# Silu by tanh in late shared experts, and final tiles moved among shared tiles, in a one-core mixture-of-experts kernel

## What is computed

```python
# cond: two shared experts, and eight routed ones of which two count for a token
for e in range(2):
    h = silu(x @ s_w1[e].T) * (x @ s_w3[e].T)
    shared = shared + h @ s_w2[e].T
for e in range(8):
    h = gelu(x @ r_w1[e].T, approximate=False)
    routed = routed + h @ r_w2[e].T * gates[:, e:e + 1]
c = (shared / 2 + routed) / 4
# ffn, of low rank
P = c @ U1
H = gelu_tanh(P @ V1 + b1)
out = (H @ U2) @ V2 + b2
```

## Time and profile before

| | |
|---|---|
| median of three runs | 882.41 us |
| the profiled execution | 882.33 us |
| its span, first to last instruction | 880.1 us |
| PE busy, 3838 matmuls | 868.8 us, 99% |
| DVE, ACT, POOL busy | 675.8, 573.0, 404.3 us |
| granted PE clock, mean | 0.999 |

### The profile page before, as it was taken

One profiled execution on the slowest core, in us unless ns is written; L12 is line 12 of the kernel. 1 busy time (PEld: TensorE's weight loads), 2 busy tenths in 40 slices (PEclk: granted clock), 3 DMA queues, 4 the chain that ended last, 5 costly groups with the idle time before them and its releaser, 6 DMA issues.

```text
span 880.1 us, 12608 instructions
## 1 busy us (share of the span) xinstructions
PE 868.8 (99%) x3838; PEld 691.6 (79%) x3838; DVE 675.8 (77%) x1091; ACT 573.0 (65%) x1029; POOL 404.3 (46%) x377
## 2 busy tenths in 40 slices
PE   8999999999999999999999999999999999999997
PEld 5787888778888888888888888888888887777874
DVE  7877777878689687686687686686665788998887
ACT  7888888755555455555555555555555678989796
POOL 7457783134356453252252252352324427754462
PEclk9999999999999999999999999999999999999999
DMA  9689981023113112012012012011010038462700
GB/s 322 216 270 308 298 288 46 1 86 136 49 48 124 43 42 84 1 48 84 1 49 83 1 49 84 0 48 49 1 48 1 1 122 211 91 182 58 158 13 36
DMA packets 36547, 83.21 MB, mean 95 GB/s; under 512 B 4480, under 2 KB 14592, under 8 KB 34688
## 3 DMA queue, kind: packets, MB, share of 16 engines
q1 hardware_dynamic: 36192, 82.15, 29.3%
q10 hardware_dynamic: 288, 0.26, 0.1%
HBM read 71.39 MB, written 6.83 MB: 89 GB/s over the span
## 4 chain that ended last, share of the span: by engine, by line
PE 70%; DVE 2%; issue 2%; ACT 2%; POOL 0%; POOLq 0%; DVEq 0%; ACTq 0%
PE ps L933 15%; PE ps L952 15%; PE ps L938 15%; PE ps L993 6%; PE ps L995 6%; PE ps L988 6%; PE ps L975 2%; PE ps L973 2%; DVE Hf L1575 1%; ACT HH L1093 1%; PE ps L968 1%; DVE HL L1588 1%; DVE HH L1585 0%; ACT Hf L1080 0%; POOL HL L1683 0%
## 5 line engine op out<-in xcount | busy, mean ns | idle before, releaser
L1087 ACT ACTIVATE Sg<-ps 128x512 f32<-128x512 f32 x288 | 171.8, 597 | 245.9 <-PE ps L952 245.3
L1568 DVE TENSOR_TENSOR Hf<-ps,Sg 128x512 f32<-128x512 f32 x288 | 198.0, 688 | 148.9 <-ACT Sg L1087 92.4
L1683 POOL TENSOR_TENSOR HL<-Hf,HH 128x512 fp32r<-128x512 f32 x133 | 177.7, 1344 | 174.5 <-ACT HH L1093 158.4
L1093 ACT ACTIVATE HH<-Hf 128x512 fp32r<-128x512 f32 x344 | 215.0, 625 | 14.2 <-DVE Hf L1568 9.8
L1588 DVE TENSOR_TENSOR HL<-Hf,HH 128x512 fp32r<-128x512 f32 x243 | 214.1, 881 | 4.3 <-ACT HH L1093 3.2
L933 PE MATMUL ps<-XHL,WBH 128*128 128x512 f32 x512 | 203.5, 397 | 0.5 <-DVE Hf L1568 0.5
L952 PE MATMUL ps<-XHL,WBH 128*128 128x512 f32 x512 | 202.1, 395 | 0.0
L938 PE MATMUL ps<-XHL,WBL 128*128 128x512 f32 x512 | 202.0, 395 | 0.0
L1698 POOL TENSOR_TENSOR XT<-XT,TMP 128x512 f32<-128x512 f32 x64 | 83.8, 1310 | 223.3 <-DVE TMP L1435 223.1
L933 PEld LDWEIGHTS ps<-XHL,WBH 128*128 128x128 f32 x512 | 96.0, 188 | 24.6 <-DVE Hf L1568 1.6
L952 PEld LDWEIGHTS ps<-XHL,WBH 128*128 128x128 f32 x512 | 96.0, 188 | 23.0
(11 more groups left out here) (261 smaller groups left out, 1325.3 us busy)
## 6 DMA issues: line engine op xcount, KB each, us to landing
CWB<-scratch SPq DMA_DIRECT2D x14, 1024.0 KB, 4.6
GWD<-expert_down SPq DMA_DIRECT2D x21, 576.5 KB, 4.6
GWU<-expert_up SPq DMA_DIRECT2D x21, 514.0 KB, 5.2
CWB<-scratch SPq DMA_DIRECT2D x40, 256.0 KB, 5.9
ST<-in_wb_dram SPq DMA_DIRECT2D x8, 768.0 KB, 6.3
ST<-scratch SPq DMA_DIRECT2D x24, 256.0 KB, 8.8
GX<-XT SPq DMA_DIRECT2D x68, 64.0 KB, 2.9
XT<-in_x_dram SPq DMA_DIRECT2D x8, 256.0 KB, 5.7
```

Of the source, the lines that this page charges most:

```text
L1087: e.activation(Sg[:, it.n % NG, :], zb[z % NZ][:, :], ACT.Silu).then_inc(s_act, 1)
L1093: e.activation(HH[:, it.n % NH, 0:it.cols], hidden_place(it), ACT.Copy).then_inc(s_hi_act, 1)
L1568: e.tensor_tensor(Hf[:, it.n % NS, :], zb[z % NZ][:, :], Sg[:, it.n % NG, :], ALU.mult).then_inc(s_prod, 1)
L1683: e.tensor_tensor(HL[:, it.n % NH, :], Hf[:, it.n % NS, :], HH[:, it.n % NH, :].bitcast(F32), ALU.subtract).then_inc(s_lo_pool, 1)
```

## The change

- `LATE` is 6 and `MIXED` is 4. At the end stand only (5, 2), (5, 3) and blocks 6 and 7: ten final tiles. (5, 0) and (5, 1) come before the routed tiles of pair 6.
- In pairs 4 and 6 the four final tiles of block b - 2 stand among the shared tiles, as S S F S S F S S F S S F. The final tiles of block b - 1 follow (four in pair 4, two in pair 6), then the routed ones. Pair 2 keeps its order.
- Whole are only (5, 3), (6, 1), (6, 3), (7, 1), (7, 3). Before, they were these and (2, 3), (3, 3), (5, 1).
- Final tiles of blocks 2 and 4 are `among`: their gelu stays in the PSUM bank, ACT makes the high part, DVE the low part, and the bank is free when that low part is made. They use no `Hf` buffer, so `hf_free` passes over them.
- Shared tiles of blocks 4 to 7 are `tanh`: ACT writes tanh(z / 2), DVE makes (tanh + 1) times z in place, which frees the gate's bank, waits for that, and multiplies by the up half. This is twice the silu, so `FOLD` scales the shared part by 0.0625. The shared tiles of blocks 0 to 3 keep the silu, and their product gets a factor of 2 by another kind of instruction.
- The low parts of all shared tiles from block 2 on are POOL's; before, blocks 2 and 3 alone. Low parts of final tiles 1 and 3 of blocks 2 to 4, as far as they had one, go from POOL to DVE. Of the final tiles at the end, the one low part that is POOL's is that of (7, 0) and no longer of (6, 0).

```diff
@@ -15,7 +15,8 @@
 BLK = 512
 NBLK = NT // BLK
 SEG = (0, 42, 86, 128)
-LATE = NBLK - 3
+LATE = NBLK - 2
+MIXED = 4
 LAG = 5
 NH = LAG + 1
 NS = 6
@@ -72,8 +73,11 @@
         self.kind, self.blk, self.ex, self.f, self.last = kind, blk, ex, f, last
         self.cols = GROUPS[blk][1] * P if kind == "G" else BLK
 
-        self.whole = kind == "F" and (f % 2 == 1 if blk >= LATE else blk in (2, 3) and f == 3)
-        self.inplace = kind in "AG"
+        self.late = kind == "F" and (blk, f) >= (LATE - 1, 2)
+        self.whole = self.late and f % 2 == 1
+        self.among = kind == "F" and blk in range(MIXED - 2, LATE, 2)
+        self.inplace = kind in "AG" or self.among
+        self.tanh = kind == "S" and blk >= MIXED
 
 
 class Order:
@@ -111,13 +115,12 @@
         return [Item("F", blk, 0, f, f == 3) for f in range(4)]
 
     for b in range(0, NBLK, 2):
-        items += shared(b) + shared(b + 1)
-        for f in (b - 2, b - 1):
-            if 0 <= f < LATE:
-                items += final(f)
-        items += routed(b) + routed(b + 1)
-    for b in range(LATE, NBLK):
-        items += final(b)
+        mixed = {"S": shared(b) + shared(b + 1), "F": final(b - 2) if b else []}
+        for kind in "SSFSSFSSFSSF" if b >= MIXED else "SSSSSSSS" + "FFFF" * (b > 0):
+            items.append(mixed[kind].pop(0))
+        items += ([it for it in final(b - 1) if not it.late] if b else []) + routed(b) + routed(b + 1)
+    for b in range(LATE - 1, NBLK):
+        items += [it for it in final(b) if it.late]
     return items
 
 
@@ -223,6 +226,7 @@
         s_small = sem("s_small")
         s_act = sem("s_act")
         s_prod = sem("s_prod")
+        s_half = sem("s_half")
         s_gated = sem("s_gated")
         s_hi_act, s_hi_dve = sem("s_hi_act"), sem("s_hi_dve")
         s_lo_dve, s_lo_pool = sem("s_lo_dve"), sem("s_lo_pool")
@@ -345,12 +349,14 @@
                 for j in range(2 if it.kind in "BS" else 1):
                     it.z.append(len(z_users))
                     z_users.append((it, j))
-        n_prod, n_gated = {}, {}
+        n_prod, n_gated, n_half = {}, {}, {}
         hi, lo = {}, {}
         n_hi_act = n_hi_dve = n_lo_dve = n_lo_pool = 0
         for it in real:
             if it.kind in "BS":
                 n_prod[it.n] = len(n_prod) + 1
+            if it.tanh:
+                n_half[it.n] = len(n_half) + 1
             if it.kind == "R":
                 n_gated[it.n] = len(n_gated) + 1
             if it.whole:
@@ -358,10 +364,10 @@
                 lo[it.n] = s_down, it.n + 1
                 continue
             it.hi_act = it.kind in "BS" or (it.kind in "AG" and it.k % (8 if it.k < 16 else 4) != 0) or (
-                it.kind == "F" and it.blk < LATE and it.k % 2 == 1) or (it.kind == "R" and it.ex % 4 != 3)
+                it.among or (it.kind == "F" and not it.late and it.f % 2 == 1)) or (it.kind == "R" and it.ex % 4 != 3)
             it.lo_pool = (it.kind == "B" and it.k % 4 in ((1, 3) if it.ex == 7 and it.blk > 2 else (1,))) or (
-                it.kind == "F" and ((it.blk, it.f) == (LATE + 1, 0) if it.blk >= LATE else it.k % 2 == 1)) or (
-                it.kind == "R" and it.ex % 4 != 1 and (it.blk, it.ex) != (NBLK - 1, 7)) or (it.kind == "S" and it.blk // 2 == 1)
+                it.kind == "F" and ((it.blk, it.f) == (LATE + 1, 0) if it.late else it.blk < 2 and it.f % 2 == 1)) or (
+                it.kind == "R" and it.ex % 4 != 1 and (it.blk, it.ex) != (NBLK - 1, 7)) or (it.kind == "S" and it.blk >= 2)
             if it.hi_act:
                 n_hi_act += 1
                 hi[it.n] = s_hi_act, n_hi_act
@@ -389,7 +395,15 @@
                 return s_gated, n_gated[it.n]
             if it.inplace:
                 return lo[it.n]
+            if it.tanh and j == 0:
+                return s_half, n_half[it.n]
             return (s_act, it.n + 1) if j == 0 else (s_prod, n_prod[it.n])
+
+        def hf_free(it):
+            n = it.n - NS
+            while real[n].among:
+                n -= NS
+            return lo[n]
 
         def sg_free(it):
             n = it.n - NG
@@ -495,6 +509,8 @@
             if k in add_y:
                 ab_done.add(("y", add_y[k]))
             if LAG <= k < len(items) + LAG and items[k - LAG] and items[k - LAG].kind == "F":
+                if (items[k - LAG].blk, items[k - LAG].f) == (LATE, 0):
+                    ab_of["over"] = len(ab_of)
                 if items[k - LAG].new and items[k - LAG].blk < NBLK - 1:
                     ab_of["Q", items[k - LAG].blk] = len(ab_of)
             if k in split_wb:
@@ -516,6 +532,8 @@
             user = ab_user[ab_of[key] - 2]
             if user == "gl":
                 user = "t"
+            if user == "over":
+                user = "Q", LATE - 1
             if user[0] == "pick":
                 user = "B", "turn", user[1]
             if user[1:2] == ("four",):
@@ -1069,7 +1087,7 @@
                     e.wait_ge(s_z, z + 1)
                     if it.kind in "AGF":
                         if not it.inplace:
-                            e.wait_ge(*lo[it.n - NS])
+                            e.wait_ge(*hf_free(it))
                         if it.kind == "F":
                             bias = col("b1", it.f)
                         elif it.kind == "A":
@@ -1084,7 +1102,10 @@
                     else:
                         if sg_free(it):
                             e.wait_ge(*sg_free(it))
-                        e.activation(Sg[:, it.n % NG, :], zb[z % NZ][:, :], ACT.Silu).then_inc(s_act, 1)
+                        if it.tanh:
+                            e.activation(Sg[:, it.n % NG, :], zb[z % NZ][:, :], ACT.Tanh, scale=0.5).then_inc(s_act, 1)
+                        else:
+                            e.activation(Sg[:, it.n % NG, :], zb[z % NZ][:, :], ACT.Silu).then_inc(s_act, 1)
                 if 1 <= k <= len(items) and items[k - 1] and items[k - 1].hi_act:
                     it = items[k - 1]
                     e.wait_ge(*hidden(it))
@@ -1528,7 +1549,7 @@
                 if k == folded:
                     bk = ab_bank("fold")
                     e.wait_ge(*small.of("fold"))
-                    e.tensor_scalar(FOLD[:, 0:4, :], bk[:, 0:128].rearrange("p (i c) -> p i c", c=32), 0.125, None,
+                    e.tensor_scalar(FOLD[:, 0:4, :], bk[:, 0:128].rearrange("p (i c) -> p i c", c=32), 0.0625, None,
                                     ALU.mult).then_inc(s_fold, 1)
                     e.tensor_scalar(FOLD[:, 4:12, :], bk[:, 128:384].rearrange("p (i c) -> p i c", c=32), 0.25, None,
                                     ALU.mult).then_inc(s_ab, 1)
@@ -1563,15 +1584,24 @@
                     it = items[k]
                     z = it.z[1]
                     e.wait_ge(s_act, it.n + 1)
+                    if it.tanh:
+                        e.scalar_tensor_tensor(out=Sg[:, it.n % NG, :], in0=Sg[:, it.n % NG, :], scalar=1.0,
+                                               in1=zb[it.z[0] % NZ][:, :], op0=ALU.add, op1=ALU.mult).then_inc(s_half, 1)
                     e.wait_ge(s_z, z + 1)
-                    e.wait_ge(*lo[it.n - NS])
-                    e.tensor_tensor(Hf[:, it.n % NS, :], zb[z % NZ][:, :], Sg[:, it.n % NG, :], ALU.mult).then_inc(
-                        s_prod, 1)
+                    e.wait_ge(*hf_free(it))
+                    if it.kind == "S" and not it.tanh:
+                        e.scalar_tensor_tensor(out=Hf[:, it.n % NS, :], in0=Sg[:, it.n % NG, :], scalar=2.0,
+                                               in1=zb[z % NZ][:, :], op0=ALU.mult, op1=ALU.mult).then_inc(s_prod, 1)
+                    else:
+                        if it.tanh:
+                            e.wait_ge(s_half, n_half[it.n])
+                        e.tensor_tensor(Hf[:, it.n % NS, :], zb[z % NZ][:, :], Sg[:, it.n % NG, :],
+                                        ALU.mult).then_inc(s_prod, 1)
                 if k < len(items) and items[k] and items[k].kind == "R":
                     it = items[k]
                     e.wait_ge(s_act, it.n + 1)
                     e.wait_ge(f_gate[it.blk % 2][it.ex], 16 * (it.blk // 2 + 1))
-                    e.wait_ge(*lo[it.n - NS])
+                    e.wait_ge(*hf_free(it))
                     e.tensor_tensor(Hf[:, it.n % NS, :], zb[it.z[0] % NZ][:, :], gate_place(it.blk, it.ex),
                                     ALU.mult).then_inc(s_gated, 1)
                 if 1 <= k <= len(items) and items[k - 1] and not items[k - 1].whole:
```

## The result

The changed kernel takes 897.47 us (median of five runs, 895.65 to 899.48) against 882.41 before: ratio 1.017, 95% interval 1.0159 to 1.0181 (numbers in square brackets behind a ratio are such intervals). It is slower, as forecast, but by 15.1 us and not by 10.5, and so 0.7 us over the upper end of the range. The profiled execution took 897.47 too; its span is 894.8 us.

A forecast was written before the change was run, and what follows sets the result against it. The prediction took PE to bound the kernel, full in routed stages. Pair 2 +0.3, pair 4 +4.4, pair 6 +6.3 and the end -0.45 gave +10.5 on 882.33, so 892.8 us, range 887.2 to 896.8.

The forecast's parts named there:

- A: Rival, mixes of pairs 4 and 6: banks don't bind, all added waits fall away; -2.0, so 880.3 us; chance 0.05.
- A': Rival: banks don't bind and the two saved table loads count in full, 2 x 1.28; 877.7 us; chance 0.01.
- D: Rival: no difference, what a stage's start loses is made up behind it; chance 0.02.
- C: Rival: DVE's two new steps stretch beside POOL, up to 1 us in each of six chains; 898 us; chance 0.09.
- B: Rival: the chain binds but the mix's start doesn't pile up; six waits of 1.2, +6.8, 889.1 us; chance 0.24.
- waits of PE that end on POOL: Sign that would show the prediction wrong: PE waiting for POOL; POOL's added low parts were expected to be hidden.
- Start: Start of pair 4's mix: late gate banks and first low-part wait, 0.67 + 0.33 + 2.13 = 3.13 us.
- Pair 2, +0.3: Doubled product of blocks 0 to 3: 16 x 0.05, felt by PE only in pair 2; 0 to 0.4, taken as 0.3.
- Pair 6: the start, 2.47: Start of pair 6's mix: PE less far ahead of ACT than in pair 4, so 0.34 + 2.13 = 2.47 us.
- Pair 6, two tiles for 1.39: Tiles (5,0) and (5,1) moved into pair 6, where PE is full: 6 x 0.231 = 1.39 us.
- The pairs for whole tiles, -0.78: Pair 4: whole final tiles become pairs of cheaper matmuls, -0.39 each, together -0.78 us.
- The end, -0.45: The end without (5,0) and (5,1): block 7's first final tile still waits for PS, so only -0.45 us.

The follow-up runs named there:

- e1: Changed kernel, but the final tiles among shared ones write their gelu to Hf and not into the bank: 888.55 us, ratio 1.0061.
- e2: Changed kernel, but DVE takes the low part of a final tile among shared ones before the next shared tile's two steps: 892.89 us, ratio 1.011.
- e7: Kernel before, with tanh in blocks 4 to 7 and low parts of all shared tiles from block 2 on by POOL: 882.65 us, ratio 1.000.
- e6: Changed kernel with a small tanh-gelu ahead of each mix's first tanh, so the table loads there: 896.15 us, ratio 1.0157.
- after: The changed kernel itself, against the kernel before: 897.47 us, ratio 1.017.
- e3: Changed kernel with final tiles (5,0) and (5,1) back at the end, (5,1) whole: 893.5 us, ratio 1.0123.
- e8: Kernel before with only final tiles (5,0) and (5,1) moved ahead of pair 6's routed tiles, (5,1) as a pair: 884.96 us, ratio 1.0024.
- e9: Kernel before with tiles (2,3) and (3,3) as pairs and not whole: 883.1 us, ratio 1.0005.
- e5: Changed kernel with eight extra matmuls, results written over, during PE's wait for PS: 895.87 us, ratio 1.0145.
- e10: Changed kernel with its final tiles among shared ones through Hf, and (5,0), (5,1) back at the end: 885.42 us, ratio 1.0034.
- e12: Changed kernel with DVE's low part first, the table load ahead of the first tanh, and (5,0), (5,1) back at the end: 889.59 us, ratio 1.0078.
- e4: Kernel before in its old order, with only tanh in blocks 4 to 7 and the doubled product in blocks 0 to 3: 885.8 us, ratio 1.0034.

## Why the prediction was right and where it failed

**Sign and mechanism: right. The step that failed: the sum took a wait of PE to cost its own length.** Behind two of the waits PE then worked at half its clock for some 4 us, 3.2 us in all, for which the sum had no term; and two terms of pair 6 were too small by 0.85 and 0.5.

PE waits for the bank that a final tile among the shared ones keeps until DVE's low part; e1 takes that away and 8.9 us with it, e2 some 0.4 of each wait. **A** and **A'** fall: no wait of the new chain fell away, and with nine loads instead of eleven from 735 us on e7 takes as long as before. **D** falls, since nothing is made up (pair 4 is 4.48 longer). **C** falls although its number, 898, is nearest to the result: DVE's new step took 0.68 beside POOL as without it (784.24 beside POOL's 784.41; the mean of all sixteen is 0.680). **B** falls: the start does pile up. Of the signs named, "waits of PE that end on POOL" are there in small (0.5 us in two waits), as they were before; they aren't where the time went.

**Term by term, on the profiled executions:**

| | predicted | measured |
|---|---|---|
| pair 2 and before | +0.3 | -0.1 |
| pair 4 | +4.4 | +4.48 |
| pair 6 | +6.3 | +8.98 |
| end | -0.45 | +1.30 |
| outside the span | 0 | +0.4 |
| sum | +10.5 | +15.1 |

- *Pair 4.* Start 3.17 (predicted 3.13), the second wait 1.42 (1.42), the third 1.25 (1.2), behind the mix 0.80 (0.89). That the start came out so close is partly luck. I put the table load ahead of the tanh, as the silu needs it in the earlier trace rows. It came at 784.68, behind two tanhs that followed an exact gelu without a load, so the whole start fell on one wait. With the load where I had it (e6) the start is 3.6 and not 3.13. Of that, 0.35 is a thing that I can't explain: the product of the third shared tile starts at 788.88 and not at 788.53, 0.14 behind the step that it waits for, and so it does in e6 (789.19), but not in pair 6 (835.07, 0.13 behind it).
- *A price too low, one too high.* The new step took 0.68 and not 0.74; the wait on its own result 0.14 (784.92 to 785.06) and not 0.04. They nearly cancel.
- *Pair 2, +0.3.* The doubled product took 0.68 on average (sixteen of them) and not 0.05 more than the plain one; nothing was lost there.
- *Pair 6: the start, 2.47, was too small.* I took PE to be less far ahead there. Measured are 0.39 + 0.11, then 2.71 + 0.10: 3.3, as in pair 4. That is 0.85 more.
- *Pair 6, two tiles for 1.39.* Priced by their matmuls alone. In after there are 0.5 us more of waits at low parts in the routed stage (behind 867.79 and 869.59), and with these pair 6 adds up: 3.3 + 1.24 + 1.25 + 0.34 for the waits, 1.57 for the clock, 1.39 + 0.5 for the tiles, less 0.65, is 8.9 of 8.98. By whole stages e3 and e8 give the two tiles 2.9 and 2.8; e3 also lacks the waits of 0.99 in all that after has from 872.46 to 874.61, at the very end of pair 6.
- *The pairs for whole tiles, -0.78.* It holds in after, where those tiles lie elsewhere and pair 4 adds up; e9 shows that it is no price of the edit alone. By itself it gives nothing.
- *The end, -0.45.* The wait for `PS` came at its place and size (2.00 + 0.08), and e8's end is 0.3 shorter. The term without the clock is nearly right: 1.30 less 1.6 is -0.3.
- *The term that was missing: the granted clock.* Twice 1.6 us, read from the distances of matmuls, so 3.2 of the 4.6 us between forecast and result. The rest is 0.85 for the start of pair 6, 0.5 for the two tiles and 0.4 outside the span, for which no run shows a reason, less 0.4 in pair 2. A wait of 2 to 3 us can thus cost 1.6 more; where it does and where not stays open, and e5 doesn't settle it.

What e8 and e3 don't settle is which of PE's small waits on POOL's low parts belongs to which moved tile; that was not tried apart.

## What to carry to other kernels

Ask of each buffer that a change keeps longer which instruction now frees it, and what stands ahead of that instruction on its engine: here a bank went from ACT's gelu to DVE's low part one slot later, and that cost most. A saved matmul is worth nothing where the engine that feeds PE is then waited for instead (e9). And a forecast for such a kernel with PE waits of 2 us or more should hold a further 0 to 1.6 us for each in its range, for the clock.

## What the runs showed of the hardware

- **The granted clock fell behind most long waits of PE, not behind all of them, and once without one.** In the profiled executions a wait of 2.5 to 3.1 us in pair 4 was followed by half clock in e5 and e6 and not in after or e3; the one in pair 6 (2.2 to 2.7) in after, e3, e5 and e6; the one at the end (2.0) in after, e1 and e2, and not in e6 or e8. In e10 and e12, with no wait over 1.3 us before PE's last matmuls, and in the mixes of e2 (up to 1.8) there was none. But in e9 it falls at 7.7 us, in the first layer, with no wait over 0.95 us since 4.7. A fall lasts some 3 to 4 us and costs about 1.6 (0.427 us from matmul to matmul and not 0.231).
- **The spread of the changed kernel, 3.8 us, is explained by the clock only in part.** Only one execution of each kernel has a profile, but the mean granted clock is known for all, and one fall takes some 0.002 off it. In e6 the four go together: 894.46 us at 0.999, 895.89 at 0.997, 896.4 at 0.996, 899.1 at 0.994. Of the changed kernel's five the slowest (899.48) has 0.994, but the fastest (895.65) has 0.996, as those at 897.23 to 897.89; and the four of e3 lie within 0.4 us at 0.995 to 0.998. What else spreads them is open.
- **Tanh needed no load, neither behind the exact gelu (781.64 in after) nor behind the final tiles' tanh-gelu (787.08).** From 735 us on ACT loads nine times and not eleven; the load at 784.68 stands ahead of the tanh-gelu (L1098), which followed an exact gelu with two tanhs between them. The Trainium skill (ScalarE: Activation LUTs, "What ACT_TABLE_LOAD costs") adds a drain to each load. The trace doesn't agree: in e6 the next activation starts at 782.83, 0.02 behind the load's end at 782.81, so no drain shows on ACT.
- **A DVE instruction that waits for the one ahead of it on DVE starts 0.14 us after that one's end** (784.92 to 785.06; 794.13 to 794.27 in e4), but for the one at 788.88 named above; without such a wait the next starts some 0.09 ahead of the end (794.96 to 794.87).
